# A second normalised-tile buffer in the tile loop, and the last stage in 512-column pieces

## The reference, cut

```python
x = u                                        # (1, 8192, 4096) float32
# attention place: a long convolution along the last axis, the same kernel K for every row
n = layernorm(x)
K = s4_kernel(Lambda, p, q, B, Ct, step, 4096)      # one vector of 4096
y = irfft(rfft(n, 8192) * rfft(K, 8192))[..., :4096] + D[0] * n
x = x + layernorm(y)
# FFN place
n = layernorm(x)
f = n @ kernel + bias + lora(n)              # 4096 x 4096 weights, rank 32 of 16 adapters + shared
x = x + layernorm(f)
```

## Time and profile before

| | us |
|---|---|
| median of 2 runs (1788.86 to 1790.85) | 1789.86 |
| the profiled execution, whole time | 1794.46 |
| its span on its slowest core (core 1) | 1792.2 |
| spans of the eight cores | 1758.6 to 1792.2 |
| mean granted TensorE clock, by core | 0.809 to 0.813 |
| TensorE busy in the span | 945.8 (53%) |
| VectorE busy | 426.4 (24%) |
| ScalarE busy | 288.2 (16%) |
| bytes moved by DMA | 149.79 MB |

### The profile page before, as it was taken

The page is one execution under the profiler, slowest core; times in us unless marked ns, Lnnn a source line. Parts: engine busy times, 40 slices in busy tenths (PEclk is TensorE's granted clock), DMA queues, the critical chain, the costliest instruction groups (busy, mean ns, idle before and its releaser), DMA issues.

```text
span 1792.2 us, 13070 instructions; the slowest of 8 cores (1758.6 to 1792.2 us)
## 1 busy us (share of the span) xinstructions
PE 945.8 (53%) x4229; PEld 423.7 (24%) x4229; DVE 426.4 (24%) x770; ACT 288.2 (16%) x378; POOL 167.4 (9%) x313
## 2 busy tenths in 40 slices
PE   5360000073655647282745899999989989300000
PEld 1010000032232323132322434334334334100000
DVE  1332442124333332424333010110110110112212
ACT  2400000213232232313132010110110110111111
POOL 0002101100000000000000123222222222000000
PEclk9999999995858767585858799989899899655555
DMA  0000635302112020202011265655555565464564
GB/s 8 1 3 11 122 60 95 89 1 94 47 47 94 1 94 1 94 1 94 22 72 47 36 106 74 105 104 73 104 107 71 103 106 71 147 220 186 210 229 193
DMA packets 66580, 149.79 MB, mean 84 GB/s; under 512 B 16727, under 2 KB 50056, under 8 KB 60576
## 3 DMA queue, kind: packets, MB, share of 16 engines
...
## 4 chain that ended last, share of the span: by engine, by line
PE 50%; DMA 18%; DVE 17%; ACT 7%; issue 6%; DVEq 1%; SPq 1%; POOL 1%; ACTq 0%; POOLq 0%
PE pffn L846 25%; PE pconv L737 15%; DMA xb<-f_scr 6%; DMA f_scr<-fstage 5%; DVE xb L763 2%; DVE ya L897 2%; DVE trv L691 2%; DVE trv L771 2%; PE ptrb L788 2%; ACT n1b L779 2%; ACT xb L894 2%; ACT n1b L699 2%; DMA trv<-lora_a 2%; DMA n1b<-lora_b 2%; PE pax L799 1%
## 5 line engine op out<-in xcount | busy, mean ns | idle before, releaser
L846 PE MATMUL pffn<-wbuf,n2fm 128*128 128x512 bf16 x2048 | 463.1, 390 | 3.2 <-DMA wbuf<-wk 3.2
L737 PE MATMUL pconv<-tband,xfmt 128*128 128x512 bf16 x1152 | 265.5, 395 | 8.5 <-DVE xfmt L720 8.5
L846 PEld LDWEIGHTS pffn<-wbuf,n2fm 128*128 128x128 bf16 x2048 | 204.1, 100 | 262.1 <-issue 33.9
L841 POOL DMA_DIRECT2D wbuf<-wk x256 | 135.2, 529 | 1062.7 <-PE pffn L846 1052.2
L863 DVE TENSOR_SCALAR_CACHE_REDUCE fstage<-pffn 128x512 f32<-128x512 f32 x64 | 44.3, 692 | 498.1 <-PE pffn L852 480.0
L737 PEld LDWEIGHTS pconv<-tband,xfmt 128*128 128x128 bf16 x1152 | 115.9, 101 | 156.2 <-issue 31.1
L867 ACT ACTIVATE tra<-fstage 128x512 bf16<-128x512 f32 x64 | 40.4, 631 | 551.5 <-DVE fstage L863 540.8
L716 PE MATMUL ptrb<-idsb,n1b 128*128 128x128 bf16 x256 | 29.5, 306 | 188.0 <-ACT n1b L699 186.4
L788 PE MATMUL ptrb<-idsb,n1b 128*128 128x128 bf16 x256 | 32.9, 310 | 167.3 <-ACT n1b L779 167.3
L741 DVE SCALAR_TENSOR_TENSOR ya<-n1b,dbc,pconv 128x512 f32<-128x512 bf16 x64 | 47.8, 747 | 225.9 <-PE pconv L737 225.9
L746 ACT ACTIVATE tra<-ya 128x512 bf16<-128x512 f32 x64 | 40.4, 630 | 275.3 <-DVE ya L741 275.3
...
## 6 DMA issues: line engine op xcount, KB each, us to landing
wbuf<-wk POOLq DMA_DIRECT2D x256, 128.0 KB, 3.0
xb<-u SPq DMA_DIRECT2D x8, 2048.0 KB, 12.1
x_scr<-xb SPq DMA_DIRECT2D x8, 2048.0 KB, 7.1
f_scr<-fstage SPq DMA_DIRECT2D x64, 256.0 KB, 3.1
xb<-x_scr SPq DMA_DIRECT2D x8, 2048.0 KB, 9.5
xb<-f_scr SPq DMA_DIRECT2D x8, 2048.0 KB, 14.0
y<-ya SPq DMA_DIRECT2D x8, 2048.0 KB, 7.3
n1b<-lora_b POOLq DMA_DIRECT2D x16, 256.0 KB, 4.0
```

The lines of the kernel that those rows point to most:

```text
L737: tg = E("tensor", lambda t, g=g, ij=ij, j0=j0: t.matmul(out=pconv[g % 3][:, :], lhsT=xfmt[:, 128 * ij:128 * ij + 128], rhs=tband[:, j0:j0 ...
L841: t_wload[kg] = DMA("gpsimd", f"wload{kg % 4}", lambda g, f=f, oc=oc, kg=kg: g.dma_start(out=wbuf[kg % 4][:, :], in_=wk[128 * f:128 * f + ...
L846: tlast = E("tensor", lambda t, f=f, t2=t2, kg=kg: t.matmul(out=pffn[t2][:, :], lhsT=bass.AP(n2fm, TOK * f + P * t2, [[FC * TOK, P], [1, P]]),
```

## The change

In the tile loop the body becomes five functions. A second bfloat16 buffer `n1c` alternates with `n1b` by tile, and a second set of LN1 statistics `st1b` with `st1`. The emission order is: load and LN1 of tile t + 1, convolution of t, `post1` of t (statistics, x1, LN2, n2), transposes of t + 1 for the convolution, `post2` of t (n2's transposes, copies, `pax` matmuls). The load of `u` for tile t + 1 also waits for n2 and the LN2 row sums of tile t - 1.

In the tail each tile's loads, normalisation, sum and store are cut into 8 pieces of 512 columns (256 KB each), with two buffers for x1 pieces (`p3b[0]`, `p3b[1]`) and two for f pieces (`p3b[2]`, `p3b[3]`), in place of `xb`. In the prologue the small tiles become slices of `p3b` and `fstage` in place of tensors of their own, with the same shapes; the instructions are otherwise the same.

The diff, cut:

```diff
...
+        n1c = e(nc.sbuf_tensor("n1c", [P, D], BF16))
...
+        p3b = [e(nc.sbuf_tensor(f"p3b{i}", [P, 512], F32)) for i in range(4)]
...
-        kt = [e(nc.sbuf_tensor(f"kt{i}", [P, 32], F32)) for i in range(16)]
...
+        kt = [p3b[0][:, 32 * i:32 * i + 32] for i in range(16)]
+        cc = [p3b[1][:, 32 * i:32 * i + 32] for i in range(6)]
+        arre = p3b[2][:, 0:32]
+        arim = p3b[2][:, 32:64]
+        c2re_s = p3b[3][:, 0:32]
...
+        wh_s = [fstage[0][0:1, :], fstage[1][0:1, :]]
...
+        st1b = stat_site("st1b")
...
+        def emit_load_ln1(t_i):
             xbt = xb[t_i % 2]
-            war = [t_x1store[t_i - 2]] if t_i >= 2 else ([t_ksum_done, t_bacc, t_bbcast] if t_i % 2 == 0 else [t_rdim, prev_ev])
-            if t_i == 0:
-                war += xb0_guard
-            if t_i == 1:
-                war += xb1_guard + [t_ksum_done]
+            st = st1p[t_i % 2]
+            nb = n1bufs[t_i % 2]
+            war = [t_x1store[t_i - 2], t_n2_tok[t_i - 2], t_rs2_tok[t_i - 2]] if t_i >= 2 else (
+                [t_ksum_done, t_bacc, t_bbcast] + xb0_guard if t_i == 0
+                else [t_rdim, prev_ev] + xb1_guard + [t_ksum_done])
             W("sync", war)
             t_uload[t_i] = DMA("sync", f"uin{t_i % 2}", lambda s, t_i=t_i, xbt=xbt: s.dma_start(
                 out=xbt[:, :], in_=u[P * t_i:P * t_i + P, :]))
-
             W("vector", [t_uload[t_i]] + (trv_guard if t_i == 0 else []))
-            t_rs = E("vector", lambda v, xbt=xbt: v.tensor_scalar(
+            t_rs = E("vector", lambda v, xbt=xbt, st=st: v.tensor_scalar(
                 out=trv[:, :], in0=xbt[:, :], scalar1=1.0, scalar2=None, op0=OP.mult, op1=OP.add,
-                accum_out=st1["s1"][:, :]))
+                accum_out=st["s1"][:, :]))
             W("scalar", [t_uload[t_i]] + (tra_guard if t_i == 0 else []))
-            t_sq = E("scalar", lambda s, xbt=xbt: s.activation(
-                out=tra[:, :], in_=xbt[:, :], func=AF.Square, accum_out=st1["q1"][:, :]))
-            t_r1, t_nb1 = ln_finalize(st1, D, t_rs, t_sq)
-            W("scalar", [t_nb1, pr.now("tensor")] + ([t_ldbs] if t_i == 0 else []) + (n1b_guard if t_i == 0 else []))
-            t_n1 = E("scalar", lambda s, xbt=xbt: s.activation(
-                out=n1b[:, :], in_=xbt[:, :], func=AF.Identity, bias=st1["nbias"][:, :], scale=st1["rstd"][:, :]))
-
-            ev_toks = []
+            t_sq = E("scalar", lambda s, xbt=xbt, st=st: s.activation(
+                out=tra[:, :], in_=xbt[:, :], func=AF.Square, accum_out=st["q1"][:, :]))
+            t_r1, t_nb1 = ln_finalize(st, D, t_rs, t_sq)
+            toks = [t_nb1]
+            if t_i >= 2:
+                toks += [t_n2tr[t_i - 2], conv_ev_last[t_i - 2]]
+            if t_i == 0:
+                toks += [t_ldbs] + n1b_guard
+            W("scalar", toks)
+            t_n1_tok[t_i] = E("scalar", lambda s, xbt=xbt, st=st, nb=nb: s.activation(
+                out=nb[:, :], in_=xbt[:, :], func=AF.Identity, bias=st["nbias"][:, :], scale=st["rstd"][:, :]))
...
+        def emit_convtransp(t_i):
+            nb = n1bufs[t_i % 2]
+            evs = []
             for r in range(4):
+                b = r % 2
+                toks = [t_n1_tok[t_i], ptrb_last[b]]
                 if t_i == 0 and r < 2:
+                    toks += [t_astk, t_kmbT] + xfmt_guard
                 W("tensor", toks)
                 tlast = None
                 for j in range(8):
                     c = 8 * r + j
+                    tlast = E("tensor", lambda t, c=c, r=r, j=j, nb=nb: t.transpose(
+                        out=ptrb[r % 2][:, 128 * j:128 * j + 128], in_=nb[:, 128 * c:128 * c + 128],
                         identity=idsb[:, :]))
+                W("vector", [tlast] + (xfmt_guard if t_i == 0 and r == 0 else []))
+                ev = E("vector", lambda v, r=r: v.tensor_copy(
+                    out=xfmt[:, 1024 * r:1024 * r + 1024], in_=ptrb[r % 2][:, :]))
+                ptrb_last[b] = ev
+                evs.append(ev)
+            ctr_ev[t_i] = evs
+
+        def emit_conv(t_i):
+            nb = n1bufs[t_i % 2]
             conv_ev = [None] * 8
             for g in range(8):
-                toks = [ev_toks[-1], t_tband]
+                toks = [ctr_ev[t_i][3], t_tband]
                 if g >= 3:
                     toks.append(conv_ev[g - 3])
-                elif last_convevac is not None:
-                    toks.append(last_convevac)
-                elif t_i == 0:
+                elif t_i > 0:
+                    toks.append(conv_ev_last[t_i - 1])
+                else:
                     toks += [t_ksum_done, gb_toks[-1]]
                 W("tensor", toks)
...
                 W("vector", [tg] + ([pr.now("scalar")] + (ya_guard if t_i == 0 else []) if g == 0 else []))
-                conv_ev[g] = E("vector", lambda v, g=g: v.scalar_tensor_tensor(
-                    out=ya[:, 512 * g:512 * g + 512], in0=n1b[:, 512 * g:512 * g + 512],
+                conv_ev[g] = E("vector", lambda v, g=g, nb=nb: v.scalar_tensor_tensor(
+                    out=ya[:, 512 * g:512 * g + 512], in0=nb[:, 512 * g:512 * g + 512],
                     scalar=dbc[:, :], op0=OP.mult, in1=pconv[g % 3][:, :], op1=OP.add,
                     accum_out=yacols[:, g:g + 1]))
...
+        def emit_post1(t_i):
...
-            W("scalar", [t_nb2, conv_ev[7]])
-            t_n2 = E("scalar", lambda s, xbt=xbt: s.activation(
-                out=n1b[:, :], in_=xbt[:, :], func=AF.Identity, bias=st2["nbias"][:, :], scale=st2["rstd"][:, :]))
-
+            W("scalar", [t_nb2, conv_ev_last[t_i]])
+            t_n2_tok[t_i] = E("scalar", lambda s, xbt=xbt, nb=n1bufs[t_i % 2]: s.activation(
+                out=nb[:, :], in_=xbt[:, :], func=AF.Identity, bias=st2["nbias"][:, :], scale=st2["rstd"][:, :]))
...
+        def emit_post2(t_i):
+            nb = n1bufs[t_i % 2]
+            last = None
             for r in range(4):
-                toks = [t_n2, ev_toks[(r + 2) % 4]]
-                W("tensor", toks)
+                b = r % 2
+                W("tensor", [t_n2_tok[t_i], ptrb_last[b]])
...
+        emit_load_ln1(0)
+        emit_convtransp(0)
+        for t_i in range(TT):
+            if t_i + 1 < TT:
+                emit_load_ln1(t_i + 1)
+            emit_conv(t_i)
+            emit_post1(t_i)
+            if t_i + 1 < TT:
+                emit_convtransp(t_i + 1)
+            emit_post2(t_i)
+        last_axmm = t_n2tr[TT - 1]
+        last_convevac = conv_ev_last[TT - 1]
+        last_ptrb_evac = ptrb_last[1]
...
-                    war = [t_p1v, t_p1a, t_x1store[TT - 1]]
-                    war += [t_fst[o2 * TT + t_i] for o2 in range(8)]
-                    if t_i >= 1:
-                        war.append(t_yst[t_i - 1])
-                    W("sync", war)
-                    t_x1l = DMA("sync", "x1in", lambda s, t_i=t_i: s.dma_start(
-                        out=xb[0][:, :], in_=x1_scr[P * t_i:P * t_i + P, :]))
-                    t_fl = DMA("sync", "fin", lambda s, t_i=t_i: s.dma_start(
-                        out=xb[1][:, :], in_=f_scr[P * t_i:P * t_i + P, :]))
...
                     t_rf, t_nbf = ln_finalize(stf, D, t_fs, t_fq)
-                    W("scalar", [t_nbf, t_fl])
-                    t_lnf = E("scalar", lambda s: s.activation(
-                        out=xb[1][:, :], in_=xb[1][:, :], func=AF.Identity, bias=stf["nbias"][:, :], scale=stf["rstd"][:, :]))
-                    W("vector", [t_lnf, t_x1l] + ([t_yst[t_i - 1]] if t_i >= 1 else []))
-                    t_add = E("vector", lambda v, t_i=t_i: v.scalar_tensor_tensor(
-                        out=ya[:, :], in0=xb[0][:, :], scalar=nall[:, t_i:t_i + 1], op0=OP.add,
-                        in1=xb[1][:, :], op1=OP.add))
-                    W("sync", [t_add])
-                    t_yst[t_i] = DMA("sync", "yout", lambda s, t_i=t_i: s.dma_start(
-                        out=y_out[P * t_i:P * t_i + P, :], in_=ya[:, :]))
-        W("sync", [t_yst[TT - 1]])
+                    rec_f = pr.dsems[f"frow{t_i}"]
+                    t_frow_all = (rec_f[0], rec_f[1])
+                    for pc in range(8):
+                        i3 = t_i * 8 + pc
+                        par = i3 % 2
+                        xbuf = p3b[par]
+                        fbuf = p3b[2 + par]
+                        war = [t_p1v, t_p1a, t_x1store[TT - 1], t_frow_all]
+                        if i3 >= 2:
+                            war.append(p3_stt[i3 - 2])
+                        W("sync", war)
+                        t_x1l = DMA("sync", f"x1i{par}", lambda s, t_i=t_i, pc=pc, xbuf=xbuf: s.dma_start(
+                            out=xbuf[:, :], in_=x1_scr[P * t_i:P * t_i + P, 512 * pc:512 * pc + 512]))
+                        t_fl = DMA("sync", f"fi{par}", lambda s, t_i=t_i, pc=pc, fbuf=fbuf: s.dma_start(
+                            out=fbuf[:, :], in_=f_scr[P * t_i:P * t_i + P, 512 * pc:512 * pc + 512]))
```

(75 more changed lines are left out.)

36 lines of the change are left out of this document (12 added, 24 removed).

## The result

The changed kernel takes 1959.93 us (median of 11 runs, 1941.15 to 1973.61) against 1789.07 for the kernel before (10 runs). The ratio is 1.094, with a 95% interval from 1.090 to 1.098: slower by 9.4%. The prediction said slower, 1884 us, with a range up to 1955. The sign and both mechanisms came out as forecast; the time lies 76 us above the forecast and 5 above the range.

A forecast was written before the change was run, and what follows sets the result against it. Waits bound the tile loop (a strict sequence) and the tail (DMA, ScalarE, VectorE taking turns), TensorE the FFN. 1794.5 + 152 (tail) - 58 (loop) = 1888.5, the median 4.6 lower: 1884 us, range 1835 to 1955.

The forecast's parts named there:

- both mechanisms: Tile loop: reordered emission gains 58 us; tail: 64 serial round trips of small pieces cost 152 us.
- The order of SP's queue: Tail: next loads queue behind the wait for the present sum, so buffer sets never overlap: 64 full round trips.
- The tile loop: Period falls from 81.4 to 69.9 us, gaining 79 us, less 21 for the clock: 58 (44 to 79).
- The stall: Convolutions 0 to 6: TensorE stands about 3.4 us after 24 matmuls, as group 0's copy waits for LN1(t+1).
- The clock: Tile loop: the stall drops TensorE from 2.4 to 1.2 GHz, losing 3 us in each of seven convolutions, 21 us.
- The rival that the clock stays up: Tile loop: no clock fall in the stall, loop gain 79 us, time 1863 us; chance 0.22.
- The load of u: Tile loop: u(t+1) loads only after n2(t-1); landing taken as 11.3 us, where VectorE comes free in any case.
- The sum c: Tail: one piece's round trip, 5.9 us (4.85 to 7.2), 64 times; tail +152 us (+84 to +235).
- The landing: Tail: f piece of 256 KB with 256 KB ahead lands 3.0 us after issue; ends 2.57 and 4.0.
- The f store ahead of each tile's first piece: Tail: each later tile's first piece waits for its f store, 2.57 plus about 0.5 us; 24 us over seven tiles.
- The case of dearer pieces: Tail: eight cores load small pieces at once, landing 4.0, c = 7.2, time 1967 us; chance 0.14.
- The FFN: Stage after the tile loop, bound by TensorE, 539.7 us; predicted to stay at 540 us.

The follow-up runs named there:

- e1: The changed kernel with the old tail (whole 4096-column loads, sum and store per tile): 1717.5 us, ratio 0.959.
- e8: The changed kernel with load and LN1 of tile t + 1 emitted behind group 3 of convolution t, not ahead of group 0: 1917.5 us, ratio 1.067.
- e10: The changed kernel with x1 and f scratches contiguous by piece and no y stores but the last two: 1852.4 us.

## Why the prediction was right, and where it missed

**The order of SP's queue**, the step on which the sign hung, held. Within a tile the x1 load goes out 0.59 us behind the y issue (predicted 0.60), two buffer sets never overlap, and issuing ahead gave at least 181 us back.

**The tile loop** held: gain 58 predicted, 63 in the stage and 72 in e1's time. The stall is where it was put, behind the 24th matmul and released by the copy of group 0. It was 4.7 us in the tile shown and 3.8 on average (26.3/7), against 3.4. The clock did fall, to 0.50 over 446 to 452: the 120 matmuls behind the stall took 27.75 to 28.7 us, 27.95 on average, against the 25.7 that the old kernel needed (convolution from 525.82 on for 33.58 us, less 7.86 for its first 24). That is 2.2 us lost per tile and not 3, or 15 us and not 21, which is the 5 us between the 58 and the 63. The rival that the clock stays up is refuted here, and e8 shows the price of stall and clock together, 39 us in the time and 43 in the tile loop. The load of u landed in 8.4 us at the median, less than the 11.3 assumed, and cost nothing, as VectorE was the later of the two.

**The tail's trip** was mis-sized, and this is the whole miss. The mean trip within a tile was 6.8 to 7.4 us on the cores. The sum c = 5.9 us had these terms, with what the trace and the runs showed:

| term | predicted | measured |
|---|---|---|
| sum's end to y issue | 0.07 | 0.08 |
| y issue to x1 issue | 0.60 | 0.59 |
| x1 issue to f issue | 0.37 | 0.37 |
| f issue to landing, median by core | 3.0 | 3.6 to 4.0 |
| landing to ScalarE | 0.15 | 0.14 |
| ScalarE, 512 columns | 0.65 | 0.813 |
| ScalarE to VectorE | 0.29 | 0.32 |
| VectorE, 512 columns | 0.75 | 0.751 |

Two failed. ScalarE's 0.65 leaned on L867, a Square without operands for scale and bias; 0.813 is outside even the upper end of 0.75 that I gave, and makes 10 us over 64 pieces. The landing was taken as an undisturbed pair's. e10 shows that such a pair does land in 2.9 us; what I left out was traffic of the piece itself, its y store and the strided rows, and core 3, the slowest, where every second landing is 4.7 us on average. The tail stage (481.1) exceeds the predicted 252.2 + 152 by 77 us. ScalarE is 10 of them. The f store ahead of each tile's first piece landed in 2.04 and not in 2.57 plus the 0.5 that I added, which took 7 back. The other 73 are the landings: core 3's mean is 4.14 us, 1.14 more than 3.0 for each of 64. On the six cores without the alternation it is about 3.8, which is 51 us of the 73; the alternation is the rest. I had the 4.0 of the lora_b load as the upper end and chose near the lower one, although each piece has two neighbours in the queue that the bare store didn't have. The Trainium skill's fit for a DMA ("DMA: Bandwidth & Descriptors", "Anatomy of one DMA"), from which I had estimated 3.2 us from x1's issue, agrees with e10's undisturbed pair (0.37 + 2.9) and not with the changed kernel's 0.37 + 3.7: it has no term for neighbours in flight.

**The range** failed for the same reason: the landing. The case of dearer pieces came nearest, with 1967, and 0.14 was too little for it, but its price is partly luck. It put all terms at their high ends (c = 7.2) and the landing at 4.0 because eight cores load small pieces at once; the runs show the piece's own neighbours, and none was made that could show what the other cores add. The FFN, put at no change, was 7 us shorter on core 3, which is scatter among cores: from its first to its last matmul it took 533.6 to 540.4 us on the eight cores before and 530.5 to 536.6 after. The 9 us between the profiled execution (1950.8) and the median (1959.93) lie in the spread of the runs.
